# A routed-expert transformer block on one core: fixed expert weights kept in SBUF for both passes, zeroing at one transfer a pair, normalising on three engines

## The reference, cut to what matters

```python
h = _layernorm(x) * (1 + ca) + sa
x = x + ga * attn(h)                       # 16 heads of 64, softmax(q k^T * scale + bias) v, output projection
h = _layernorm(x) * (1 + cb) + sb
probs = sigmoid(h @ router_w.T + expert_bias)
top_w, top_idx = top_k(probs, 8)           # weights of the 8 are normalised and scaled by 2.5
h1 = silu(einsum('th,eih->eti', h, w_gate))            # 160 experts, 128 -> 64
routed = einsum('eti,ehi->th', h1 * combine.T[:, :, None], w_down)   # 64 -> 128
shared = silu(h @ w_gate_shared.T) @ w_down_shared.T
x = x + gb * (routed + shared)
```

## Time and profile before

| | us |
|---|---|
| median of 3 runs (951.09 to 961.61) | 959.02 |
| the profiled execution | 956.92 |
| its span, first to last instruction | 955.1 |
| PE busy in the span | 742.6 |
| POOL busy | 612.7 |
| DVE busy | 550.1 |
| ACT busy | 461.6 |

### The profile page before, as it was taken

How to read it: one execution, slowest core, us unless ns; L and a number is a source line. 1 busy time by engine, 2 the same in 40 slices (tenths; PEclk the granted TensorE clock), 3 DMA queues, 4 the chain that set the end, 5 groups by cost and what they waited for, 6 DMA issues and landing times. The chain is left out here.

```text
span 955.1 us, 15917 instructions
## 1 busy us (share of the span) xinstructions
PE 742.6 (78%) x5132; PEld 527.9 (55%) x5132; DVE 550.1 (58%) x1400; ACT 461.6 (48%) x960; POOL 612.7 (64%) x495
## 2 busy tenths in 40 slices
PE   4889979999899999999899949978577786880000
PEld 2656656666566666666665537767466675660000
DVE  5867746775577777776776744635222554552343
ACT  3666646667656557766578704423233342340000
POOL 0688858887678777887877857406513777005775
PEclk9999989999899999999999978979778998885555
DMA  7989978878573525444353338989999999972221
GB/s 228 246 252 282 340 202 256 261 231 273 178 219 74 126 67 124 125 116 113 83 137 104 122 142 270 409 316 328 346 301 332 371 354 372 335 262 94 52 63 49
DMA packets 92821, 204.31 MB, mean 214 GB/s; under 512 B 14546, under 2 KB 36500, under 8 KB 89156
## 3 DMA queue, kind: packets, MB, share of 16 engines
q1 hardware_dynamic: 76484, 157.15, 54.7%
q10 hardware_dynamic: 8064, 29.36, 7.8%
q0 software_dynamic: 8192, 16.79, 5.7%
HBM read 112.48 MB, written 68.22 MB: 189 GB/s over the span
## 5 line engine op out<-in xcount | busy, mean ns | idle before, releaser
L1181 POOL TENSOR_SCALAR prob<-prob,rinv 128x512 f32<-128x512 f32 x228 | 356.0, 1572 | 109.9 <-DVE rinv L1375 107.2
L993 ACT ACTIVATE prob<-prob,nmax 128x512 f32<-128x512 f32 x256 | 182.9, 715 | 151.7 <-DVE nmax L1357 150.9
L1198 POOL DMA_INDIRECT sorted_rows<-xn,dest x128 | 126.2, 986 | 87.5 <-issue 87.5
L320 DVE COPY PT<-ps 128x512 f32<-128x512 f32 x128 | 88.3, 690 | 140.9 <-PE ps L570 140.1
L1357 DVE CUSTOM_DVE_ANT_0 prob<-ps,strips 128x512 f32<-128x512 f32 x256 | 164.8, 682 | 0.5 <-issue 0.2
L570 PEld LDWEIGHTS ps<-ident,prob 128*128 128x128 f32 x1024 | 115.7, 142 | 77.8 <-POOL prob L1181 42.5
L570 PE MATMUL ps<-ident,prob 128*128 128x128 f32 x1024 | 138.6, 279 | 4.6 <-ACT PT L320 3.8
L1238 POOL DMA_INDIRECT stack<-sorted_rows,dest x64 | 61.9, 967 | 106.1 <-DMA sorted_rows<-prob 87.2
L583 PE MATMUL ps<-PT,v_sb 128*64 128x512 f32 x512 | 123.8, 605 | 5.0 <-ACT PT L320 4.9
L1775 DVE COPY v_sb<-ps 128x512 f32<-128x512 f32 x56 | 38.6, 690 | 136.4 <-PE ps L859 136.3
L559 PE MATMUL ps<-stack 128*128 128x512 f32 x256 | 113.8, 444 | 2.9 <-DVE nmax L1357 2.9
(11 more groups left out here) (212 smaller groups left out, 1042.2 us busy)
## 6 DMA issues: line engine op xcount, KB each, us to landing
stack<-qk SPq DMA_DIRECT2D x128, 256.0 KB, 3.9
sorted_rows<-in_zero_rows SPq DMA_DIRECT2D x28, 1024.0 KB, 7.6
wT<-sorted_rows SPq DMA_DIRECT2D x56, 512.0 KB, 6.5
sorted_rows<-prob ACTq DMA_DIRECT2D x38, 512.0 KB
strips<-in_expert_rows SPq DMA_DIRECT2D x128, 96.0 KB
strips<-in_L_ffn_w_gate SPq DMA_DIRECT2D x40, 256.0 KB
strips<-in_L_ffn_w_down SPq DMA_DIRECT2D x40, 256.0 KB
sorted_rows<-woT ACTq DMA_DIRECT2D x18, 512.0 KB
```

What stands on the lines that cost most here:

```text
L320: return copy(dst[:, :, qt * P:(qt + 1) * P], ps[:, BANK_T + u % 2, :].rearrange("p (k s) -> p k s", s=P))
L993: nc.scalar.activation(prob[:, u, :], prob[:, u, :], ACT.Exp, bias=nmax[:, u:u + 1], scale=-1.0, accum_out=rsum[:, u:u + 1]).then_inc(s_ex ...
L1181: nc.gpsimd.tensor_scalar(prob[:, u, :], prob[:, u, :], rinv[:, u:u + 1], None, ALU.mult).then_inc(s_prob, 1)
L1198: nc.gpsimd.indirect_dma_start(sorted_rows[g], bass.IndirectOffsetOnAxis(ap=dest[:, n, k:k + 1], axis=0), rows[:, n, :], None).then_inc(s_ ...
```

## The change

The ring of known weights goes. All 20 sets have a place of their own in SBUF (`known_weights`), each in a tile that is free by then: strips of the bias, `PT`, `prob`, `hT`. Each is read once, by one transfer of 512 KB with 4 KB per partition instead of two with 2 KB, and serves both groups. Four of them (14 to 17) go through a copy in DRAM first (`late_rows`, one transfer of 2 MB). Sets 0 to 3 are read in pair 31 as before; 12 to 15, 18 and 4 to 7 follow as their tiles come free at the end of attention, 8 to 11 after the first six blocks, 16, 17 and 19 in iteration 15. The first chosen weights are now issued ahead of the first blocks. The wait for a used buffer is gone from the loop.

`fill` issues one transfer a pair over 28 pairs, after `stack_pair`, and each group's zeroing has a semaphore of its own. Three units a pair go to ACT in pairs 21 to 27 (before two); from pair 28 on four go to ACT, one to DVE and three to POOL (before four and four from pair 29). POOL scatters five a pair in pairs 21 to 27 (before four), four in pair 28, and eight a pair from pair 29 (before seven).

```diff
-    return (3, 7) if pair < 3 * HPAIRS + 5 else (1, 3, 5, 7)
+FIRST_SCATTER, SECOND_SCATTER = 2 * HPAIRS + 5, 3 * HPAIRS + 4
+def normaliser(pair, u):
+    if pair < FIRST_SCATTER:
+        return ON_POOL
+    if pair < SECOND_SCATTER:
+        return ON_ACT if u in (1, 3, 7) else ON_POOL
+    return ON_ACT if u % 2 == 1 else ON_DVE if u == 2 else ON_POOL
...
             for b in range(B - 1):
                 for n in range(2, HPAIRS + 2):
-                    fill(2 * (b * HPAIRS + n - 2))
-                    fill(2 * (b * HPAIRS + n - 2) + 1)
                     if n == HPAIRS - 2:
...
                     stack_pair(b, n + 2)
                     if b == 0 and n + 3 < HPAIRS:
                         load_strips(n + 3)
+                    fill(b * HPAIRS + n - 2)
             for n in range(2, HPAIRS - 2):
                 stack_pair(B - 1, n + 2)
+                fill((B - 1) * HPAIRS + n - 2)
+            sp.dma_start(late_rows, known_rows[:, LATE[0] * 1024:(LATE[-1] + 1) * 1024]).then_inc(s_late, 16)
...
             def load_known(k):
-                if k >= len(KNOWN):
+                if k in LATE:
+                    at = (k - LATE[0]) * 1024
+                    sp.wait_ge(s_late, 16)
+                    sp.dma_start(known_weights[k], late_rows[:, at:at + 1024]).then_inc(s_known[k], 16)
                     return
-                first = STEPS[KNOWN[k]][1]
-                if k >= NKNOWN:
-                    sp.wait_ge(s_down, KNOWN[k - NKNOWN] + 1)
-                r = k % NKNOWN
-                sp.dma_start(weights[:, r, 0:STEP * I], gate_t_in[:, first * I:(first + STEP) * I]).then_inc(s_known[r], 16)
-                sp.dma_start(weights[:, r, STEP * I:2 * STEP * I],
-                             down_pairs[:, first * I:(first + STEP) * I]).then_inc(s_known[r], 16)
+                sp.dma_start(known_weights[k], known_rows[:, k * 1024:(k + 1) * 1024]).then_inc(s_known[k], 16)
...
             sp.wait_ge(s_ttr, B * G)
             sp.dma_start(iota, block_iota).then_inc(ld["iota"], 16)
+            sp.wait_ge(s_t, B * G)
+            load_known(12)
+            load_known(13)
+            sp.wait_ge(s_cex, 1)
+            sp.wait_ge(s_matched, 2)
+            load_known(14)
+            load_known(15)
+            load_known(18)
+            sp.wait_ge(s_pv, B * HPAIRS)
+            for k in range(4, 8):
+                load_known(k)
+            load_chosen(0, range(STEP))
             for s in range(NX):
                 load_blocks(s)
-            load_chosen(0, range(STEP))
+            for k in range(8, 12):
+                load_known(k)
             load_chosen(1, range(STEP))
             for s in range(len(STEPS)):
                 load_blocks(s + NX)
-                if s in KNOWN:
-                    load_known(KNOWN.index(s) + NKNOWN)
+                if s == 15:
+                    sp.wait_ge(s_cex, 2)
+                    load_known(16)
+                    load_known(17)
+                    load_known(19)
...
-                        elif at >= SECOND and u % 2 == 0:
-                            more = 1 if u == 6 else 2
-                            scatter(1, sent, sent + more)
-                            sent += more
+                        if FIRST_SCATTER <= at < SECOND_SCATTER and u in (0, 2, 4, 5, 6):
+                            scatter_more(0, 1)
+                        elif at > SECOND_SCATTER and u % 2 == 0:
+                            scatter_more(1, 2)
+                        elif at == SECOND_SCATTER and u >= 6:
+                            scatter_more(1, 2)
```

More of the change, by code:

```diff
@@ L86 @@
 CHOSEN = [s for s, step in enumerate(STEPS) if step[2]]
-NX, NKNOWN, NCHOSEN, NY, NGATHER = 6, 4, 2, 3, 8
+NX, NCHOSEN, NY, NGATHER = 6, 2, 3, 8
+KNOWN_STEPS = E // STEP
+LATE = range(14, 18)
 RANK_UNIT = 512
@@ L232, in adaln_block @@
         h2T = yT
-        weights = strips[:, 5376:9472].rearrange("p (r n) -> p r n", r=NKNOWN)
+        known_weights = tuple(
+            [strips[:, 5376 + n * 1024:6400 + n * 1024] for n in range(4)] + [work[:, n * 1024:(n + 1) * 1024] for n in range(8)]
+            + [prob[:, u:u + 2, :].rearrange("p u n -> p (u n)") for u in (2, 6)]
+            + [flat_hT[:, at, :].bitcast(F32) for at in (1, 2, 3, 0)] + [strips[:, 0:1024], strips[:, 1792:2816]])
         chosen_weights = strips[:, 9472:12544].rearrange("p (r n) -> p r n", r=NCHOSEN)
@@ L294, in adaln_block @@
         s_sg, s_ss, s_sd, s_base = sem("shared_gate"), sem("shared_silu"), sem("shared_down"), sem("shared_added")
+        s_late = sem("late_rows_copied")
         s_x = [sem(f"blocks_loaded{r}") for r in range(NX)]
-        s_known = [sem(f"weights_loaded{r}") for r in range(NKNOWN)]
+        s_known = [sem(f"weights_loaded{k}") for k in range(KNOWN_STEPS)]
         s_chosen = [sem(f"chosen_weights_loaded{r}") for r in range(NCHOSEN)]
@@ L474, in _ @@
             sp.wait_ge(s_ttr, (B - 1) * G + (HPAIRS - 1) * UNITS)
-            for k in range(NKNOWN):
+            for k in range(4):
                 load_known(k)
@@ L867, in weights_of @@
                     return chosen_weights[:, k % NCHOSEN, :], (s_chosen[k % NCHOSEN], 16 * STEP * (k // NCHOSEN + 1))
-                k = KNOWN.index(s)
-                return weights[:, k % NKNOWN, :], (s_known[k % NKNOWN], 32 * (k // NKNOWN + 1))
+                k = STEPS[s][1] // STEP
+                return known_weights[k], (s_known[k], 16)
             def gate(s):
@@ L1194, in scatter @@
                     pool.wait_ge(s_dest, b + 1)
-                    pool.wait_ge(s_fill, 16 * sum(-(-group.width // NT) for group in GROUPS))
+                    pool.wait_ge(s_fill[g], 16 * -(-GROUPS[g].width // NT))
                 for i in range(first, end):
@@ L1206, in _, with scatter_more @@
             pool.wait_ge(s_half, 1)
-            FIRST, SECOND = 2 * HPAIRS + 5, 3 * HPAIRS + 5
-            sent = 0
+            sent = [0, 0]
+            def scatter_more(b, count):
+                end = min(sent[b] + count, SCATTERS)
+                scatter(b, sent[b], end)
+                sent[b] = end
             for b in range(B):
@@ L1931 @@
     a = {n: np.asarray(inputs[n]) for n in _LAYOUT}
+    gate, down = np.asarray(inputs["L0_ffn_w_gate"]), np.asarray(inputs["L0_ffn_w_down"])
     given = [(n, np.ascontiguousarray(lay_out(a[n]) if lay_out else a[n])) for n, lay_out in _LAYOUT.items()]
```

59 lines of the change are left out of this document (33 added, 26 removed).

## The result

The changed kernel takes 923.62 us (median of 4 runs, 916.72 to 925.52) against 957.09 (951.09 to 961.61): ratio 0.9641, 95% interval 0.9565 to 0.9717. The forecast was 911 with a range of 890 to 934. The profiled execution took 924.12 us with a span of 922.3, before 956.9 and 955.1.

What follows compares the result with a forecast made beforehand. PE was taken to bound attention; in the steps, whichever of transfers, batch 3's scatter chain or DVE's combination ends last. 956.9 - 9 + 1.5 - 4 - 11 - 6.5 - 17 = 910.9, forecast 911 us, range 890 to 934.

Steps and rivals of the forecast that it cites:

- Part 1: Attention, pairs 6, 14 and 22: less zeroing ahead of `hcur` shortens PE's waits, 9 us less, bounds 4 and 13.
- Part 2: End of attention: moved normalising and scattering cost nothing beside PE, except a POOL scatter gap in pair 31; 1.5 us more.
- Part 3: Attention's end to gate(4): first block read 2 us sooner, gate(4)'s wait for known weights saves 2; 4 us less.
- Part 4: Steps 4 to 14: SP freed, chosen weights come about a step earlier, gate(11)'s wait and half clock go; 11 us less.
- Part 5: Step 14 to gate(26): batch 3's scatter chain shortens in gap, landing and SP's order behind it; 6.5 us less, bounds 0 and 10.
- The sign that batch 3's first scatter comes 22 us earlier: Steps: POOL's first scatter of batch 3 some 22 us earlier would show the forecast right, with gate(26) still waiting for it.
- Part 6: Group 1, from gate(28): waits for weights and the lower clock behind them shrink; 17 us less, bounds 8 and 28.7.
- More is not to be had from transfers, because DVE ends last: Group 1: DVE's combinations, not transfers, limit the gain; three steps take 13.5 us whatever the transfers do.
- Transfers throughout: Rival: transfers are the bound everywhere, so group 1 shortens by all bytes no longer read, 28.7 us; total 899, chance 0.16.
- Late chosen weights: Rival in the steps: chosen weights stay late, the 36.6 us of waits stay; total 934, chance 0.20.
- they did not stay in full: Rival in attention: PE still waits for `hcur` in full, 7 us lost again; 918, counted within the forecast's 0.58.
- the slower case: Rival in the steps: SP's register reads for chosen experts become the bound; 1,047 us, chance 0.03.

Runs made afterwards that it cites:

- second profile: The changed kernel itself, unedited, timed and profiled again: 920.38 us, ratio 0.9658 to the kernel before.
- Experiment 2: Changed kernel with the zeroing transfer ahead of `hcur` at the three batch changes issued behind it and that pair's stacking: 916.55 us, ratio 0.9599.
- Experiment 1: Changed kernel with zeroing, normalising and scattering as before the change, only the weights kept resident: 932.28 us, ratio 0.9752.
- experiment 3: Changed kernel with the first six block reads issued ahead of the first eight chosen experts: 918.44 us, ratio 0.9634.
- experiment 9: Changed kernel with the first six block reads ahead of the first chosen weights and four known sets behind those weights: 927.33 us, ratio 0.97.
- experiment 7: Changed kernel with batch 3's sigmoid replaced by a linear function, so ACT loads no table around it: 918.48 us, ratio 0.9612.
- experiment 6: Changed kernel with chosen weights issued ahead of the block read that waits for batch 3's scatters: 916.51 us, ratio 0.960.
- Experiment 8: Changed kernel with the 20 no longer read sets of known weights copied memory to memory, no step waiting for them: 930.81 us, ratio 0.9759.
- Experiment 4: Changed kernel with DVE's combination cut into three parts, one beside each of three steps: 917.61 us, ratio 0.9641.

## Why the prediction came out as it did

The direction, the order of size and the range were right; the point was 12.6 us low (9.4 by the second median). The forecast stages add up to 46 us; 32.8 came in the first profile and 35.6 in the second. Ahead of gate(4) 7.8 of the missing 13.2 us lie in the first and 7.9 of 10.4 in the second; steps 4 to 14 miss 4.6 in the first and 1.0 in the second. So the misses that stay are in attention and at the hand-over, where I counted 7.5 + 4 us and 3.8 + 0 came.

- **Part 1, zeroing (9 less).** The two gaps gave it: pairs 6 and 14 won 3.6 and 4.5 us, and pairs 7 and 15 behind them 0.5 and 0.4, 9.0 in sum (8.7 in the second profile), although `hcur` took 6.8 to 7.3 us to land and not 6.5. What failed is pair 22: I had 0.2 us, and it lost 1.6 (3.0 in the second profile). PE arrives there 7.3 us earlier, but `hcur` is issued only 6.0 earlier. Of that difference 0.74 us are the issue of the zeros ahead, which my sum for that pair left out. The landing then took 0.8 more than my 6.5. Experiment 2 shows what was to be had: 12.4 at the three pairs, near my outer bound of 13.
- **Part 2, normalising (1.5 more).** The size was about right by luck, for the cause was wrong. No scatter gap struck pair 31; pairs 23, 27 and 28 became 0.6, 0.3 and 1.2 us longer. Experiment 1, which takes the new shares of work away, has the old lengths; experiment 2, which takes the waits for `hcur` away and keeps the shares, has the new ones. At pair 28 PE waits 1.33 us for ACT's copy (0.74 before), so "at nothing" failed for ACT. What is left of attention's miss, 1.2 us, lies in pair 0 and is not in the second profile. That DVE's four normalisations cost the scatters nothing held: three of the four lie beside a scatter, and these scatters took 0.96 to 1.01 us; the longest of all 128 is 1.31 us, before 1.24. The Trainium skill (SBUF — State Buffer, "A bandwidth-pool intuition that's wrong (but worth ruling out)") has a transfer of about 620 ns take about 3100 ns beside a DVE copy. No scatter here shows such a stall.
- **Part 3, the hand-over (4 less).** Three terms failed. From attention's end to the first block read SP took 12.0 us instead of the 10.6 I had worked out: the read came 4.35 us earlier, 3.8 of it attention's, so 0.55 of my 2 us were left. From the read to PE's first transposes it then took 4.5 us instead of 3.7, which I had in the range and not in the point. Experiments 3 and 9 show the three layers: SP's order, then the queue of known sets, then the later block. The Trainium skill (DMA: Bandwidth & Descriptors, "🔬 Queues, rings and completion order") says that each DMA engine takes descriptors in ring order. 3.7 us to landing with five sets ahead (experiment 9) and 7.5 with nine (experiment 3), issued at the same distance from pair 31, agree. The other 2 us, for gate(4), were put down to known weights, as the trace named them; experiment 7 shows that they are ACT's two table loads. The Trainium skill (ScalarE: Activation LUTs, "What ACT_TABLE_LOAD costs") gives 1283 ns for such a load. The trace has 1.28 us.
- **Part 4, steps 4 to 14 (11 less).** 6.4 and 10.0 in the two profiles. The mechanism was right: gate(11)'s wait went from 7.59 us to 2.09, and to nothing in the second profile, where nearly the whole forecast came.
- **Part 5, batch 3's scatters (6.5 less).** 8.5 and 6.8. Right, with the shorter landing as worked out; gate(26) still waits for them, and experiment 6 shows that much of this wait was SP's order. The sign that batch 3's first scatter comes 22 us earlier failed (10.1, 639.78 against 649.87): it adds up parts 1 to 4, with their misses.
- **Part 6, group 1 (17 less).** 15.2 and 17.9. The size was right, and its largest term too: gate(28) to gate(33) takes 20.8 us, where I had 21.3. "More is not to be had from transfers, because DVE ends last" was half right. Experiment 8 puts some 6.6 to 9.3 us of the gain down to the bytes and the other 8.6 to waits and order, a split that is rough for the reason given there. Experiment 4 shows that with DVE out of the way transfers end last at once, with nothing gained.
- **The rivals.** Transfers throughout (28.7 us in group 1) fell with the 15.2 to 17.9 measured and in experiment 8. The Trainium skill (SBUF — State Buffer, the same section) holds that HBM is almost always the bound end to end. By that rule 29 us would have come off in this stage, by the prediction's estimate. Late chosen weights would have kept 36.6 us of waits, and 20.3 are left. At pairs 6 and 14 the waits for `hcur` fell from 8.75 us to 3.50; they did not stay in full. SP's register reads have a median of 0.274 us: nothing of the slower case.

What stays open: where the rest of experiment 6's 6.4 us at gate(28) goes, since group 1 varies by 5.9 us between profiles with the same code in it; what holds gate(20); and how much of experiment 8's cost is its writes.

## What to carry to other kernels

When a stage has two candidates for what ends last, take one away on the chip before counting on the other's gain: here taking away nearly 10 us of waits for DVE brought 9 us of waits for chosen weights. A transfer moved out of the way is still ahead of something in its queue, so follow the next reader down the queue, and redo every later clock time with what the earlier parts shift. A wait that the profile puts down to a transfer can be another engine's: look whether it is still there when the transfer is gone.

## What the runs showed of the hardware

POOL's scatters have gaps 28 issues apart. In all fourteen profiles there is one ahead of the 29th and the 57th of the 64 scatters of batches 2 and 3: 2.1 to 6.7 us and 3.3 to 6.8 us, with 0.30 us between the others of a batch (the 6.77 and 4.84 us quoted are the second of them). Their cause was not tried. Over all profiles `hcur` lands 3.8 to 5.3 us after its issue with no zeros ahead, 6.6 to 7.8 with one transfer and 8.4 to 9.8 with two.
